# Attention stage rewritten: Pool only scatters rows, the routing is merged, and VectorE and ScalarE drain between dependent operations

## What is computed

```python
def attention(input, adj, W, a):
    h = input @ W
    s1, s2 = h @ a[:F, 0], h @ a[F:, 0]
    e = leaky_relu(s1[:, :, None] + s2[:, None, :], 0.2)
    e = where(adj > 0, e, -9e15)
    return elu(softmax(e, axis=2) @ h)

x = x + attention(layernorm(x), adj, W, a)
gate = layernorm(x) @ Wg.T + bg
topk_scores, topk_idx = top_k(gate, 2)
topk_probs = softmax(topk_scores)
x = x + sum of topk_probs[k] * expert[topk_idx[k]](layernorm(x))
x = x + gru(layernorm(x), adj)          # 3 layers
x = x + moe16(layernorm(x))
```

## Time and profile before

| | us |
|---|---|
| median of 3 runs | 1330.41 (1330.07 to 1338.6) |
| the profiled execution | 1332.74 |
| its span, first to last instruction | 1331.0 |
| attention stage, to the experts' first load | 276.9 |
| mean granted TensorE clock over the span, as a share of full speed | 0.857 |

### The profile page before, as it was taken

The page is one execution under the profiler, slowest core; times in us unless marked ns, Lnnn a source line. Parts: engine busy times, 40 slices in busy tenths (PEclk is TensorE's granted clock), DMA queues, the critical chain, the costliest instruction groups (busy, mean ns, idle before and its releaser), DMA issues. The chain is left out here.

```text
span 1331.0 us, 28510 instructions
## 1 busy us (share of the span) xinstructions
PE 1012.3 (76%) x6752; PEld 816.7 (61%) x6753; DVE 805.5 (61%) x3187; ACT 566.6 (43%) x1436; POOL 629.5 (47%) x686
## 2 busy tenths in 40 slices
PE   3655665459999999299987979879861799999930
PEld 2544544359999999245544545545431799888830
DVE  5777677536566666347776867768652444444427
ACT  3555545224343433146544645546431333333325
POOL 3567767725555555301334253352545266666540
PEclk8766666579999999699989989889975799999975
DMA  4222331222222221122202032040003222222229
GB/s 117 67 74 82 86 97 38 63 71 70 69 69 71 69 69 54 60 64 64 77 20 88 8 95 81 14 128 8 30 27 81 74 82 79 83 79 81 70 85 323
DMA packets 126206, 98.74 MB, mean 74 GB/s; under 512 B 33864, under 2 KB 115400, under 8 KB 126152
## 3 DMA queue, kind: packets, MB, share of 16 engines
q1 hardware_dynamic: 105536, 61.24, 16.9%
q0 software_dynamic: 17152, 35.29, 8.1%
q10 hardware_dynamic: 3464, 1.59, 0.5%
HBM read 55.44 MB, written 42.62 MB: 74 GB/s over the span
## 5 line engine op out<-in xcount | busy, mean ns | idle before, releaser
L1435 POOL DMA_INDIRECT result<-e_y,e_ids x280 | 281.8, 1007 | 247.6 <-PE e_ps_h L1464 103.4
L1464 PE MATMUL e_ps_h<-e_xT,e_up_of 128*128 128x128 f32 x2240 | 281.5, 279 | 14.4 <-DVE e_hT L1558 9.2
L1464 PEld LDWEIGHTS e_ps_h<-e_xT,e_up_of 128*128 128x128 f32 x2240 | 266.9, 195 | 20.4 <-issue 16.0
L1479 PE MATMUL e_ps_y<-w_sb,e_hT 128*128 x1664 | 209.5, 276 | 0.7 <-ACT e_y L1516 0.6
L1479 PEld LDWEIGHTS e_ps_y<-w_sb,e_hT 128*128 128x128 f32 x1664 | 197.5, 192 | 1.2 <-issue 1.2
L375 POOL DMA_INDIRECT queue<-g_q_rows,g_q_slots x128 | 129.0, 1008 | 77.8 <-DVE g_q_gap L320 38.1
L375 POOL DMA_INDIRECT queue<-a_r_rows,a_r_slots x128 | 128.2, 1001 | 66.4 <-issue 43.8
L1532 DVE COPY e_up_of<-w_sb 128x512 f32 x280 | 114.7, 449 | 3.4 <-issue 0.9
L1558 DVE TENSOR_TENSOR e_hT<-e_ps_h,e_gate 128x512 f32<-128x512 f32 x72 | 49.4, 686 | 111.3 <-ACT e_gate L1512 108.4
L1503 ACT ACTIVATE e_hT<-e_ps_h,b_sb 128x128 f32<-128x128 f32 x272 | 77.6, 368 | 87.4 <-PE e_ps_h L1464 78.9
L1490 ACT ACTIVATE e_xT<-e_ps_x 128x256 f32<-128x256 f32 x140 | 56.4, 403 | 110.7 <-PE e_ps_x L1452 103.5
(11 more groups left out here) (218 smaller groups left out, 1894.1 us busy)
## 6 DMA issues: line engine op xcount, KB each, us to landing
e_xq<-queue SPq DMA_DIRECT2D x280, 64.5 KB
g_y<-result SPq DMA_DIRECT2D x16, 512.0 KB
o_y<-result SPq DMA_DIRECT2D x16, 512.0 KB, 5.3
w_sb<-w SPq DMA_DIRECT2D x48, 128.0 KB
result<-e_y,e_ids POOLq DMA_INDIRECT x280
x_res<-x SPq DMA_DIRECT2D x16, 256.0 KB
w_sb<-w SPq DMA_DIRECT2D x16, 256.0 KB
out<-x_res SPq DMA_DIRECT2D x16, 256.0 KB, 4.6
```

Of the source, the lines that this page charges most:

```text
L1435: pool.indirect_dma_start(out=result, out_offset=bass.IndirectOffsetOnAxis(ap=ids[at_down.k][:, t, :].bitcast(U32), axis=0), in_=y[at_down ...
L1464: last = pe.matmul(ps_h[b][:, t, q * P:(q + 1) * P], up_of[at_up.k % 4][:, t, q * P:(q + 1) * P], xT[at_up.k % 4][:, t, :], start=True, st ...
L1479: last = pe.matmul(ps_y[b][:, t * D:(t + 1) * D], hT[at_down.k % 4][:, t, q * P:(q + 1) * P], down[:, bass.ds(e * (chunks * P) + q * P, P) ...
```

## The change

The mathematics is the same; the stage is written anew:

- **Steps.** `five_deep` becomes `staged`: four steps written out, a loop of three passes with four steps each, four steps written out. Again 20 steps, with five groups in flight. The rows have four buffers, not two.
- **Pool** runs only the eight scatters of g4. The inverse standard deviation is now made by ScalarE as Ln (with EPS as bias), a drain, then Exp with scale -0.5; VectorE makes the shift with one operation.
- **Logits.** Both halves of the logits and the mask are now products of TensorE, added up in PSUM: two products of 64x256 as before, eight new ones of 64x64 (float32), and one of the identity with the bf16 mask (128x256). ScalarE copies the sum to SBUF (`e`); VectorE no longer adds the two terms and the mask.
- **Row sums** come as a 129th column of the mix (a column of ones in `h`), so the reduction over 512 columns (L715) goes. The ELU is `min(exp(z), 1) + max(z, -1)`, with the shift of 1 put into `h`; L656 goes.
- **Routing** of both ranks at once: one comparison, one product, one reduction where there were two each; the cast of the indices and the cast of the slots go; the ranks are 5 bf16 products, not 14, and stand after the projection, ahead of the score product. The second copy of the rows goes, as the second normalisation writes into the rows. The probabilities (exp, add, reciprocal, product) are made once for all 64 tiles at the end.
- **Waits.** On VectorE and ScalarE a drain stands between dependent operations in place of the semaphore, also in `tile_table` (both of its uses).
- **Loads.** All loads of `x` and `adj` are issued early, `adj` has a buffer of its own for each group, and the next block's weights follow as two large transfers.

The core of it:

```diff
+    for j in range(TURN):
+        step(0, j)
+    with eng.Fori(1, NG // TURN) as i:
+        for j in range(TURN):
+            step(i, j)
+    for j in range(4):
+        step(NG // TURN, j)
...
     def link(instruction):
-        count_of[0] += 1
-        instruction.then_inc(b.step, 1)
-        v.wait_ge(b.step, count_of[0])
+        v.drain()
...
         @block.vector
...
             def body(g0, g1, g2, g3, g4):
                 if g2:
+                    wait(v, QA, "mixed", g2.s)
+                    v.reciprocal(halves(rinv[:].unsqueeze(2)), half_o[:, :, :, D:D + 1])
+                if g0:
+                    v.wait_ge(here, g0.s + 1)
+                    stats(norm1, VN1, g0.s)
+                if g2:
+                    v.drain()
+                    v.tensor_tensor(halves(z[:]), half_o[:, :, :, 0:D], halves(bc(rinv[:], D)), ALU.mult).then_inc(VU.sem, 1)
+                if g1:
+                    wait(v, AE, "e", g1.s)
+                    v.scalar_tensor_tensor(out=e[:], in0=e[:], scalar=0.2, in1=e[:], op0=ALU.mult, op1=ALU.max)
+                if g0:
+                    aggregate(norm1, VN1, g0.s)
+                if g1:
+                    v.drain()
+                    v.tensor_reduce(rowmax[:], e[:], AX.X, ALU.max)
...
+                if g1:
+                    v.drain()
+                    v.tensor_tensor(e[:], e[:], bc(rowmax[:], N), ALU.subtract).then_inc(VA.sem, 1)
+                if g0:
+                    shift(norm1, VN1, AN1, g0.s)
+                if g3:
+                    wait(v, QR, "scored", g3.s)
+                    v.tensor_tensor(score[:], ...)
...
         @block.scalar
...
+            def inverse_std(m, V, A, s):
+                wait(act, V, "agg", s)
+                act.activation(m.log[:], m.mv[:, :, 1], ACT.Ln, bias=eps[:])
+                act.drain()
+                act.activation(m.rstd[:], m.log[:], ACT.Exp, scale=-0.5).then_inc(A.sem, 1)
...
                 if g0:
                     wait(act, QX, "h", g0.s)
+                    wait(act, QA, "mixed", g0.back(2))
+                    act.activation(h[g0.b % 2][:, :, 0:D], ps_h[:]..., ACT.Copy, bias=-1.0).then_inc(AH.sem, 1)
+                    wait(act, QX, "s", g0.s)
+                    act.activation(e[:], ps_s[:, 0:G * N]..., ACT.Copy).then_inc(AE.sem, 1)
...
         @block.tensor
...
+                if g3:
+                    wait(pe, VS, "both", g3.s)
+                    pe.matmul(ranks_ps, c.before[:], both[:]..., start=True, stop=False)
+                    for u in range(G):
+                        last = pe.matmul(ranks_ps[:, (u + 1) * E0:(G + 1) * E0]..., c.ones[:], ...)
+                    last.then_inc(QK.sem, 1)
+                if g0:
+                    wait(pe, VM, "neg", g0.s)
+                    wait(pe, AE, "e", g0.back(1))
+                    for q in range(2):
+                        pe.matmul(ps_s[q * N:(q + 1) * N, 0:G * N], wa_wide[1][:], xnT[:]..., start=True, stop=False)
+                    for q in range(2):
+                        for t in range(G):
+                            pe.matmul(ps_s[q * N:(q + 1) * N, t * N:(t + 1) * N],
+                                      xnT[:, t * P + q * N:t * P + (q + 1) * N], wa_wide[0][:],
+                                      start=False, stop=False)
+                    pe.matmul(ps_s[:, 0:G * N], ident_b[:], neg[g0.b % 2][:]..., start=False, stop=True).then_inc(QX.sem, 1)
```

More of the change, by code:

```diff
@@ L130, in program @@
         c.half_made = ctx.enter_context(nc.semaphore("half_made"))
+        c.pad_made = ctx.enter_context(nc.semaphore("pad_made"))
         c.constants_made = ctx.enter_context(nc.semaphore("constants_made"))
@@ L540, in gat_and_routing @@
+        both = sb("both", [P, G + 1, E0], BF16)
+        rank = sb("rank", [P, G, E0])
+        pick = sb("pick", [P, TOPK, G, E0])
+        slots = [sb(f"slots{b}", [P, TOPK, G], U32) for b in range(TURN)]
+        rows = [sb(f"rows{b}", [P, TOPK, G, ROW]) for b in range(TURN)]
+        gap, den = sb("gap", [P, NT]), sb("den", [P, NT])
         table = table_buffers(sb, sem, E0)
         ps_t = pb("ps_t", [P, GN])
-        ps_h = pb("ps_h", [P, 2, GN])
-        ps_s = pb("ps_s", [P, G * N])
+        ps_h = pb("ps_h", [P, GN])
@@ new lines, in body @@
+                    wait(pool, AC, "rows", g4.s)
+                    alone(pool, c)
+                    for k in range(TOPK):
+                        for t in range(G):
+                            pool.indirect_dma_start(
+                                out=c.queue0,
+                                out_offset=bass.IndirectOffsetOnAxis(ap=slots[g4.b][:, k, t:t + 1], axis=0),
+                                in_=rows[g4.b][:, k, t, :], in_offset=None).then_inc(queued[g4.b], 16)
+            staged(pool, body)
@@ new lines, in stats, with aggregate, shift @@
+            def stats(m, V, s):
+                for t in range(G):
+                    v.bn_stats(m.stats[:, t, :], c.x[:, s * G + t, :])
+            def aggregate(m, V, s):
+                v.drain()
+                for t in range(G):
+                    last = v.bn_aggr(m.mv[:, t, :], m.stats[:, t, :])
+                last.then_inc(V.sem, 1)
+            def shift(m, V, A, s):
+                wait(v, A, "rstd", s)
+                v.scalar_tensor_tensor(out=m.shift[:], in0=m.mv[:, :, 0], scalar=-1.0, in1=m.rstd[:],
+                                       op0=ALU.mult, op1=ALU.mult).then_inc(V.sem, 1)
@@ new lines, in body @@
+                if g3:
+                    v.drain()
+                    for t in range(G):
+                        v.max_index(where[:, t, :], top[:, t, :], score[:, t, :])
+                if g2:
+                    v.drain()
+                    stats(norm2, VN2, g2.s)
+                if g3:
+                    v.drain()
+                    v.tensor_tensor(hot[:], c.iota_e[:, None, None, 0:E0].to_broadcast([P, TOPK, G, E0]),
+                                    bc(where[:, :, 0:TOPK].rearrange("p t k -> p k t"), E0),
+                                    ALU.is_equal)
@@ new lines, in body @@
+                if g2:
+                    aggregate(norm2, VN2, g2.s)
+                if g3:
+                    v.tensor_tensor(gap[:, bass.ds(g3.s * G, G)], top[:, :, 1], top[:, :, 0], ALU.subtract)
+                    v.drain()
+                    v.tensor_tensor(both[:, 0:G, :], hot[:, 0, :, :], hot[:, 1, :, :], ALU.add).then_inc(VS.sem, 1)
+                if g2:
+                    shift(norm2, VN2, AN2, g2.s)
+                if g3:
+                    carry = c.carry[:, 0:E0]
+                    wait(v, QK, "ranked", g3.s)
+                    v.tensor_tensor(rank[:], ranks_ps[:, 0:G * E0].rearrange("p (t e) -> p t e", t=G),
+                                    carry[:, None, :].to_broadcast([P, G, E0]), ALU.add)
+                    v.drain()
+                    v.tensor_tensor(carry, ranks_ps[:, G * E0:(G + 1) * E0], carry, ALU.add).then_inc(VK.sem, 1)
+                    v.tensor_tensor(pick[:], hot[:], rank[:, None, :, :].to_broadcast([P, TOPK, G, E0]),
+                                    ALU.mult)
+                    v.drain()
+                    with nc.allow_low_precision(reason="one term of each sum is not zero, a whole number"):
+                        v.tensor_reduce(slots[g3.b][:], pick[:], AX.X, ALU.add).then_inc(VK.sem, 1)
```

410 lines of the change are left out of this document (199 added, 211 removed).

## The result

The changed kernel takes **1349.74 us** (median of 4 runs, 1346.46 to 1352.98), before in the same rounds 1330.24: a ratio of **1.0137** with a 95% interval of 1.0084 to 1.0190. The forecast was 1316.5, range 1291 to 1342. So it is slower by 1.4%, outside the range, on a side that I had given 0.13.

A forecast was written before the change was run, and what follows sets the result against it. No engine was full; a chain across VectorE, ScalarE and TensorE plus loop stalls set the pace. Start 25.0, fourteen steps 170.8, stalls 14.7 + 3.3, then 28.6 and 20.6: gain 13.9, so 1316.5 us, range 1291 to 1342.

The forecast's parts named there:

- The stalls: Attention stage: 4.9 us for each loop pass, 14.7 in place of 24.5, and 3.3 ahead of the loop.
- The pace T: Period of a step in the attention stage, taken as 12.2 us, between 11.2 and 14.0.
- The drains: Drains between dependent operations on VectorE and ScalarE: 0.04 us each, 0.1 as the dearer case.
- two ways to fail first: The forecast fails first if a drain costs much more than 0.04 us or the stalls aren't the loop's.
- Pool: Scatters in the attention stage: a floor of 10.4 us a step, waiting 1.5 to 2 us a step for slots.
- The rival by which relief counts in full: Attention stage: the step falls to Pool's floor of 10.4 us, 25.2 us less, 1291; chance 0.12.
- TensorE's product at the low clock (T = 14): Attention stage: the longer score product sets a step of 14.0 us, 25.2 more, 1342; chance 0.16.
- A body of four steps that stalls twice: Attention stage's loop: 9.8 us of stalls a pass, 14.7 more, 1331; chance 0.15.
- the loop theory: Waits without a releaser come once a loop pass, from the instruction stream after a jump, 4.9 us each.
- Tables: ScalarE switches tables between Ln and Exp: four loads a step, 71 us more, near 1390; chance 0.04.
- The ends: Attention stage: step 2 begins at 25.0, 28.6 us from step 16 to the last rank, 20.6 to the experts' load.
- Behind the stage: The rest of the kernel after the experts' first load: 1054.1 us, the same as before.

The follow-up runs named there:

- b_four: The kernel before with two loop passes of four steps in place of five of two, in a free hour: 1.0003 of before.
- e_filled: The changed kernel with a power on Pool behind the third and the fifth scatter, in a held hour: 1.0047 of before.
- c_semsplit: The changed kernel with semaphores for all drains and Pool's row of eight scatters cut by a wait for the mix, held hour: 1.0068 of before.
- a_split: The changed kernel with the last four of Pool's eight scatters waiting for the mix, in a free hour: 0.9826 of before.
- f_after: The changed kernel itself, nothing edited, run again in a held hour: 1.0126 of before.
- f_sems: The changed kernel with semaphores in place of all drains, in a held hour: 0.9919 of before.
- c_row8: The kernel before with Pool's powers moved ahead, so its eight scatters of a step are one row, held hour: 1.0414 of before.
- e_four: The kernel before with two loop passes of four steps in place of five of two, in a held hour: 0.9967 of before.
- a_sems: The changed kernel with semaphores in place of all drains, in a free hour: 0.9732 of before.

## Why the prediction was wrong, step by step

- **The stalls: wrong, and this decides.** The step was "Kept at 4.9 us: 14.7 in place of 24.5" under *Loop*. I had seen that the waits of the earlier trace rows come every second step and that a pass has two steps, and took the one for the cause of the other. Pool's rows have the same period, and its timeline would have shown it. The holding belongs to the scatters; the change made of rows of 3 + 3 every second step a row of eight in each. Fourteen steps took 209.1; at the pace of the free hours, 12.0, they would take 168. That is 41 us held, where I charged 18.0: the 23 us are more than the miss of the steps (20.3). The 12.0 is that of other kernels, but the changed kernel's own profiles give it too, at 11.8 to 12.2, once the excess ahead of `xnT` is taken off. In before it is 204.4 - 188 (`b_four`) = 16, where I charged 27.8. What no run shows is a changed kernel that broken rows make faster in a held hour: in both tries (`e_filled`, `c_semsplit`) the rows joined again elsewhere.
- **The pace T: right.** 12.2 was predicted; the three kernels with drains took 11.9 to 12.0 a step in free hours, before's form 13.4. Right partly by luck, since it held a term that was off by most of a microsecond (the drains) and others that made up for it:
- **The drains: too cheap.** I took 0.04 like a semaphore, with 0.1 as the upper end. For a drain between two operations that depend on each other this holds (0.03 to 0.04 above a semaphore). What the term left out is that a drain also waits for an operation that nobody needs yet: with that they cost 0.16 to 0.23 each above a semaphore on VectorE, and in the whole step 0.9 us (12.0 against 11.0 and 11.1). The prediction named this as one of two ways to fail first, and it did, along with the other. Taken alone it would have cost 14 x 0.9 = 13 us against a kernel with semaphores.
- **Pool: right in kind, not in size.** No run shows that its relief gave anything by itself. It waits 5.5 us a step instead of 1.5 to 2, because the held step is 2.7 us longer than the forecast, and because the eight scatters take 10 us and are followed by nothing. The rival by which relief counts in full (10.4 us a step) is refuted; only the kernels with semaphores came near it, in free hours.
- **TensorE's product at the low clock (T = 14): not the cause.** The score product took 1.12 + 1.51 + 0.28, 2.6 us from start to end, inside the predicted 1.7 to 3.2, and the steps are 12.0 without holding. The clock was 0.61 (0.63 over 78 to 228 us), not 0.75 to 0.85; `a_split` had 0.74 over 78 to 228 us with about the same busy time of TensorE, 98 us against 102. Why it was granted less isn't shown; little of the step can be due to it, since 11.8 to 12.2 are left without the excess ahead of `xnT`.
- **A body of four steps that stalls twice: refuted** with the loop theory, though its price (1331) was closer than mine. The Trainium skill, "Runtime: NRT & Kernel Launch", section "Instruction fetch mechanics", on which it leaned, says when a jump makes a fetch. In before no instruction packet lay in the 100 us with stalls, so the waits of the earlier trace rows, which the prediction took to agree with it, don't bear it out.
- **Tables: right.** One load in the stage, in the groups of ScalarE (the answer to the earlier trace rows):

```profile
L785 ACT ACT_TABLE_LOAD x1 | 1.3, 1283 | 0.8 <-POOL half_neg L159 0.8
```

  Ln and Exp alternate behind it with no second one. The Trainium skill, "ScalarE: Activation LUTs", section "Table sets", has both in one set; the trace agrees.
- **The ends: right within 3 us.** Step 2 at 26.3 (25.0), to the last rank 30.4 (28.6), and then SP's pads and the load, which answer:

```profile
268.60 15.67 SPq L466 DMA_DIRECT2D queue<-pad  x4
286.44 13.41 SPq L1499 DMA_DIRECT2D e_xq<-queue  x18
```

- **Behind the stage: 8.3 us that I counted as nothing.** By TensorE's first instruction of each block, the first experts take 0.9 us more, the GRU block 4.7 and the last experts 2.9. In the other three profiles of the changed kernel the rest is 1056.7 to 1058.2 us, 2.6 to 4.1 above before's. Only the tile table of the GRU block was edited there. What carries these few us isn't settled. Nor is this: in held hours the kernels with semaphores ran the GRU block in 451 to 456 us against 474 to 479 of before and the changed kernel, 20 us, while in free hours all have 439 to 448. So most of the distance between `f_after` and `f_sems` (27.7 us) lies outside the stage (their experts' loads are 1.7 us apart), and the price of the drains is to be read from the free hours alone.

**A version that beats both.** The changed kernel with semaphores in place of its drains: 0.973 and 0.976 of before in free hours, 0.992 in a held one (0.986 with ScalarE's drains kept, in another held hour). Against the changed kernel in the same session, `f_sems` has 1310.44 / 1338.09 = 0.979.

## What to carry to other kernels

A wait with no releaser is a question, not a fact about its place: before charging it to a loop, a fetch or an instruction, list what every other engine and queue does in each of its occurrences, and look for the one with the same period. When work is taken off Pool, see what it had separated: in before, to move the powers out of the row of scatters cost 54 and 61 us, in held hours (to put two back into the changed kernel's row did not shorten its step). Where two chains are woven together on one engine, a drain costs more than a semaphore, because it also waits for the other chain's operation. A break made by a wait is gone as soon as the engine has a backlog.

## What the runs showed of the hardware

- Long rows of indirect scatters from Pool (eight of 128 rows, 1.26 us apart) can hold back other engines: in `c_row8` VectorE's `z` goes on 6.7 us after the recorded end of the mix, in the changed kernel a VectorE drain lasts 1.0 us. The release comes 2.5 to 2.7 us after the start of the last scatter in these two, but also in the midst of a row (136.73 in `c_row8`, 147.75 in `c_semsplit`). Rows of six do it, too, but not each time (`e_four`). In free hours 24 in a row held nothing (`a_sems`).
- It comes and goes. In two sessions no profiled kernel had it and before took 1258 and 1260; in three others (and in the first comparison) all had it and before took 1322 to 1331. Most of the 63 to 73 us between them lie behind the attention stage: the GRU block takes 474 us in before's profile against 441 in `b_four`, the last experts 293 against 264, the first experts 284 in both. In before's trace Pool sends rows of twelve scatters in the GRU block, mostly rows of four in the last experts and of one or two in the first; that fits the rows and proves nothing. Waits without a releaser come to some 130 us in before from 300 to 1260 us, to none in `b_four`. One chip showed both. What switches it is open; every kernel of a session that I could compare shared it. A comparison must therefore have both kernels in one session, and a step's price from one hour doesn't carry to the other.
- A drain on VectorE or ScalarE between two operations of which the second has to wait for the first: 0.03 to 0.04 us above a semaphore to the engine itself. Where the operation in front is another chain's, 0.16 more (`xz` to `MAX8`); over woven stretches 0.16 to 0.23 for each drain.
- What is held, the product's last write or the report of it, the records can't tell.
